# A two-layer decoder on one core: the routings' position matrices in another layout, the first norms' roots on Pool, and fewer waits at the last stop

## The reference

```
x += attention with mixed key halves (16 heads)        # layer 0
x += cross attention over 64 context rows (16 heads)
x += experts: 8 experts of 1024, top 2 of each token, at most 320 tokens an expert
x += retention (xpos turned queries and keys, decay, group norm)   # layer 1
x += cross attention
x += experts: 8 experts, top 2, relu, no limit
```

## Time and profile before

| | us |
|---|---|
| three runs: lowest, median, highest | 1706.25, 1707.44, 1709.11 |
| the profiled execution | 1711.54 |
| its span | 1709.7 |
| PE, DVE, ACT, POOL busy | 1563.4, 977.8, 583.6, 405.6 |

### The profile page before, as it was taken

How to read it: one execution, slowest core, us unless ns; L and a number is a source line. 1 busy time by engine, 2 the same in 40 slices (tenths; PEclk the granted TensorE clock), 3 DMA queues, 4 the chain that set the end, 5 groups by cost and what they waited for, 6 DMA issues and landing times. The chain is left out here.

```text
span 1709.7 us, 31257 instructions
## 1 busy us (share of the span) xinstructions
PE 1563.4 (91%) x10625; PEld 1105.4 (65%) x10626; DVE 977.8 (57%) x1754; ACT 583.6 (34%) x1161; POOL 405.6 (24%) x544
## 2 busy tenths in 40 slices
PE   6999999999989816999999999999989949999996
PEld 5734343343467615777777777865657649999995
DVE  6678888888679775122111221378879863444443
ACT  3277777777645400111111111033446500000000
POOL 1000000000122103142322211156652103333331
PEclk9999999999999957999999999999999969999998
DMA  2112221111411111133431331200024126666674
GB/s 75 38 44 68 57 57 47 42 47 42 158 32 38 50 44 41 16 96 105 105 87 28 96 87 16 65 1 2 1 79 157 50 91 180 176 176 180 181 183 118
DMA packets 89077, 134.90 MB, mean 79 GB/s; under 512 B 17568, under 2 KB 66080, under 8 KB 88832
## 3 DMA queue, kind: packets, MB, share of 16 engines
q1 hardware_dynamic: 73824, 113.05, 21.0%
q0 software_dynamic: 15168, 20.72, 7.6%
HBM read 98.00 MB, written 20.84 MB: 70 GB/s over the span
## 5 line engine op out<-in xcount | busy, mean ns | idle before, releaser
L2163 DVE TENSOR_REDUCE mx<-ps 128x1 f32<-128x1024 f32 x256 | 300.3, 1215 | 59.1 <-PE ps L2260 59.1
L1331 PE MATMUL ps<-xTe,wide 128*128 128x320 f32 x1024 | 277.6, 433 | 1.5 <-DVE hTe L1400 0.9
L1331 PEld LDWEIGHTS ps<-xTe,wide 128*128 128x128 f32 x1024 | 194.2, 190 | 82.3 <-DVE hTe L1400 1.4
L1400 DVE TENSOR_TENSOR hTe<-prT,ps 128x320 f32<-128x320 f32 x128 | 62.4, 488 | 213.5 <-ACT prT L1372 208.3
L2062 ACT ACTIVATE wide<-ps 128x512 f32<-128x512 f32 x256 | 139.3, 599 | 64.7 <-PE ps L2269 64.7
L2062 ACT ACTIVATE turns_of_use<-ps 128x512 f32<-128x512 f32 x256 | 139.6, 601 | 59.0 <-PE ps L2269 58.9
L2269 PE MATMUL ps<-QS,KS 99*128 99x512 bf16 x512 | 153.8, 381 | 0.7 <-ACT turns_of_use L2062 0.3
L1490 PEld LDWEIGHTS ps<-xw_all,w1t 128*128 128x128 f32 x1248 | 145.3, 192 | 3.6 <-issue 1.0
L1490 PE MATMUL ps<-xw_all,w1t 128*128 128x128 f32 x1248 | 145.8, 275 | 1.2 <-issue 0.7
L1372 ACT ACTIVATE prT<-ps 128x320 f32<-128x320 f32 x128 | 56.1, 438 | 261.7 <-PE ps L1331 260.0
L1507 PE MATMUL ps<-wide,hTm 128*128 x624 | 141.0, 379 | 0.0
(11 more groups left out here) (310 smaller groups left out, 2331.1 us busy)
## 6 DMA issues: line engine op xcount, KB each, us to landing
w1t<-in_L_ffn_w SPq DMA_DIRECT2D x39, 1024.0 KB
wide<-in_L_ffn_gate_weight SPq DMA_DIRECT2D x8, 1024.0 KB
wide<-_L_ffn_ff_pre_act_weight SPq DMA_DIRECT2D x8, 1024.0 KB
wide<-L_ffn_ff_post_act_weight SPq DMA_DIRECT2D x8, 1024.0 KB
wide<-in_L_ffn_w SPq DMA_DIRECT2D x1, 8192.0 KB, 27.3
QS<-wide SPq DMA_DIRECT2D x192, 32.0 KB, 2.0
KS<-wide SPq DMA_DIRECT2D x192, 32.0 KB, 2.0
VS<-V_all SPq DMA_DIRECT2D x32, 128.0 KB, 2.1
```

The costliest lines, as they stand in the source:

```text
L1331: ins = pe.matmul(ps[:, 3 + 2 * (q % 2) + n, 0:HC], wt[:, k, f * P:f * P + P], xTe[:, k, hf * HC:hf * HC + HC], start=(k == 0), stop=(k == ...
L1400: v.tensor_tensor(hTe[:, f, hf * HC:hf * HC + HC], sgt[:, q % 2, :], ps[:, 4 + 2 * (q % 2), 0:HC], ALU.mult).then_inc(f_m.sem, 1)
L2163: v.tensor_reduce(mx[:, s, t:t + 1], ps[:, 2 * (t % 2):2 * (t % 2) + 2, :], AX.XY, ALU.max).then_inc(h_rm.sem, 1)
```

## The change

Four things change. First, `one_hot`, `id_marks`, `gate_marks` and `hi_hot` get the tile (chunk) index innermost. What the comparison reads as a repeated single element before (step 0 in the innermost dimension) is now read along 16 or 32 neighbouring elements, and the numbers that it is compared with are laid out in full by Pool, once in each layer (`pool_numbers`, into `prT`, behind the last `x_av`). PE's operands become slices with a step: 16 elements for the stationary one, 32 for the moving one. Second, at the start Pool finishes the first norms' factors, in four parts of 2, 2, 4 and 8 tiles, the counters are raised in three portions around it, the memsets beside the values come behind `a_w`, ACT issues three of the loads and writes pair 1's rows, and DVE takes the last eight tiles' statistics one pair earlier. Third, the factors of the first two tiles of the retention are finished by Pool. Fourth, at stop 4 PE, ACT and DVE raise the counter without waiting for it.

```diff
@@ buffers @@
-            .rearrange("p (k t q) -> p k t q", k=2, t=NT)
+            .rearrange("p (k q t) -> p k q t", k=2, t=NT)
-        id_marks = marks[:, 0:2 * NT * 2 * NY].rearrange("p (c n h) -> p c n h", n=2, h=NY)
-        gate_marks = marks.rearrange("p (c n h) -> p c n h", n=3, h=NY)
-        hi_hot = ....rearrange("p (c h) -> p c h", h=NY)
+        id_marks = marks[:, 0:2 * NT * 2 * NY].rearrange("p (n h c) -> p n h c", n=2, h=NY)
+        gate_marks = marks.rearrange("p (n h c) -> p n h c", n=3, h=NY)
+        hi_hot = ....rearrange("p (h c) -> p h c", h=NY)
+        numbers = prT[:].rearrange("p h q -> p (h q)").bitcast(BF16)
+        q_numbers = numbers[:, 0:P * NT].rearrange("p (q t) -> p q t", t=NT)
+        h_numbers = numbers[:, P * NT:P * NT + NY * 2 * NT].rearrange("p (h c) -> p h c", h=NY)
@@ stops @@
+        def leave(eng):
+            eng.drain().then_inc(barrier, 1)
@@ pool_cross, one turn of its loop @@
+                if i == NP:
+                    pool.wait_ge(r_iota, 1)
+                    pool_numbers(pool, c, of(layer, NP - 1))
                 if here(i - 1):
                     end_factors(pool, c, i - 1, x_fid, x_fd, of(layer, i - 1))
@@ routing @@
-        chunks = lambda m: m.rearrange("p k t -> p (k t)").unsqueeze(2).to_broadcast([P, 2 * NT, NY])
+        chunks = lambda m: m.rearrange("p k t -> p (k t)").unsqueeze(1).to_broadcast([P, NY, 2 * NT])
+        def pool_numbers(pool, c, U):
+            pool.wait_ge(x_av.sem, x_av.upto(U))
+            c(pool.tensor_copy(q_numbers, iota_b[:].unsqueeze(2).to_broadcast([P, P, NT])))
+            pool.tensor_copy(h_numbers, tiles_b[:].unsqueeze(2).to_broadcast([P, NY, 2 * NT])).then_inc(r_numbers, 1)
         def dve_ids(v, c, layer, meanwhile):
-            v.wait_ge(r_iota, 1)
-            c(v.tensor_tensor(hi_hot, tiles_b[:].unsqueeze(1).to_broadcast([P, 2 * NT, NY]), chunks(hi_b[:]),
-                              ALU.is_equal))
-            v.tensor_scalar(id_marks[:, :, 0, :], hi_hot, row_no[:, 0:1], None, ALU.mult)
-            for k in range(2):
-                v.tensor_tensor(id_marks[:, k * NT:k * NT + NT, 1, :], hi_hot[:, k * NT:k * NT + NT, :],
-                                tiles_b[:, 0:NT].unsqueeze(2).to_broadcast([P, NT, NY]), ALU.mult)
+            v.wait_ge(r_numbers, layer + 1)
+            c(v.tensor_tensor(hi_hot, h_numbers, chunks(hi_b[:]), ALU.is_equal))
+            v.tensor_scalar(id_marks[:, 0, :, :], hi_hot, row_no[:, 0:1], None, ALU.mult)
+            v.tensor_tensor(id_marks[:, 1, :, :], hi_hot, chunks(tile_of[:]), ALU.mult)
             for k, made in ((0, r_rhs), (1, r_hot)):
-                v.tensor_tensor(one_hot[:, k, :, :], iota_b[:].unsqueeze(1).to_broadcast([P, NT, P]),
-                                lo_b[:, k, :].unsqueeze(2).to_broadcast([P, NT, P]), ALU.is_equal).then_inc(made, 1)
+                v.tensor_tensor(one_hot[:, k, :, :], q_numbers, lo_b[:, k, :].unsqueeze(1).to_broadcast([P, P, NT]),
+                                ALU.is_equal).then_inc(made, 1)
@@ pe_ids (pe_gates likewise) @@
-                ins = pe.matmul(ps[:, 0, 0:2 * NY], one_hot[:, i // NT, i % NT, :],
-                                id_marks[:, i, :, :].rearrange("p n h -> p (n h)"), ...
+                ins = pe.matmul(ps[:, 0, 0:2 * NY], one_hot[:, i // NT, :, i % NT],
+                                id_marks[:, :, :, i].rearrange("p n h -> p (n h)"), ...
@@ retention, DVE and then Pool @@
-            factors(*BACK[0])
+            begin_factors(v, *BACK[0], x_fia)
+            pool.wait_ge(x_fia.sem, x_fia.upto(NP))
+            finish_factors(pool, c, *BACK[0], e_fa)
@@ start, SP and then ACT @@
-            for dst, src in ((ident[:], ...), (qwB[:], ...), (wkA, ...), (wqA, ...), (wvA, ...)):
+            for dst, src in ((ident[:], w["c_ident"]), (wkA, chunked(w["L0_attn_Wk"]))):
+            for dst, src in ((qwB[:], ...), (wqA, ...), (wvA, ...)):
+                act.dma_start(dst, src).then_inc(w_part, 16)
...
+            act.wait_ge(a_fa.sem, a_fa.upto(1))
+            act.wait_ge(a_xn.sem, a_xn.upto(0))
+            act_rows(act, 1, xn[:, 1, :, :], a_xn)
@@ start, Pool @@
-            for s in sigs:
+            for s in sigs[0:12]:
                 pool.sem_inc(s.sem, LAG * s.per)
+            def factors_of(n):
+                pool.wait_ge(a_fi.sem, a_fi.upto(n))
+                finish_factors(pool, c, (0, 2, 4, 8)[n], (2, 4, 8, 16)[n], a_fa)
+            factors_of(0)
+            factors_of(1)
+            for s in sigs[12:50]:
+                pool.sem_inc(s.sem, LAG * s.per)
+            factors_of(2)
+            pool.wait_ge(a_w, 1)
             (the memsets beside the values, as before, with v_set)
+            for s in sigs[50:]:
+                pool.sem_inc(s.sem, LAG * s.per)
+            factors_of(3)
@@ start, DVE @@
-            factors_of(0, 1)
-            ln_rows(v, 0, 0, a_xn, a_tr)
+            stats_of(0, 2)
+            stats_of(2, 4)
             v.wait_ge(w_part, W_LOADS)
             (maximum and difference of the softmax weights, as before)
+            v.wait_ge(a_fa.sem, a_fa.upto(0))
+            ln_rows(v, 0, 0, a_xn, a_tr)
...
-            ln_rows(v, 1, 1, a_xn, a_tr)
             c(v.tensor_copy(identb[:], ident[:]))
-            factors_of(1, 2)
+            stats_of(4, 8)
+            v.wait_ge(a_xn.sem, a_xn.upto(1))
             for u in range(2, NP):
-                if u == 4:
-                    factors_of(2, 4)
+                if u == 3:
+                    stats_of(8, 16)
+                v.wait_ge(a_fa.sem, a_fa.upto(2 if u < 4 else 3))
                 ln_rows(v, u, u % 2, a_xn, a_tr)
@@ stop 4, on ACT, DVE and PE @@
-            meet(..., 4)
+            leave(...)
```

More of the change, by code:

```diff
@@ L471, in row_stats @@
             return ins
-        def norm_factors(v, c, t0=0, t1=NT):
-            for t in range(t0, t1):
-                ins = v.bn_aggr(mv[:, t, :], stats[:, t, :])
-            c(ins)
-            rsqrt(v, c, nv[:, :, t0:t1], mv[:, t0:t1, 1], LN_EPS)
         def norm_rows(v, out_, t):
@@ L1186, in pe_ids @@
                     pe.wait_ge(r_hot, layer + 1)
-                ins = pe.matmul(ps[:, 0, 0:2 * NY], one_hot[:, i // NT, i % NT, :],
-                                id_marks[:, i, :, :].rearrange("p n h -> p (n h)"), start=(i == 0), stop=(i == 2 * NT - 1))
+                ins = pe.matmul(ps[:, 0, 0:2 * NY], one_hot[:, i // NT, :, i % NT],
+                                id_marks[:, :, :, i].rearrange("p n h -> p (n h)"), start=(i == 0), stop=(i == 2 * NT - 1))
             ins.then_inc(r_sum, 1)
@@ L1193, in pe_gates @@
             for i in range(2 * NT):
-                ins = pe.matmul(ps[:, 7, 0:3 * NY], one_hot[:, i // NT, i % NT, :],
-                                gate_marks[:, i, :, :].rearrange("p n h -> p (n h)"), start=(i == 0),
+                ins = pe.matmul(ps[:, 7, 0:3 * NY], one_hot[:, i // NT, :, i % NT],
+                                gate_marks[:, :, :, i].rearrange("p n h -> p (n h)"), start=(i == 0),
                                 stop=(i == 2 * NT - 1))
@@ L1730, in rows_back @@
                 c(row_stats(v, BACK[n][0], BACK[n][1] - BACK[n][0]))
-            def factors(t0, t1):
-                norm_factors(v, c, t0, t1)
-                v.scalar_tensor_tensor(out=nmr[:, t0:t1], in0=mv[:, t0:t1, 0], scalar=-1.0, in1=nv[:, 0, t0:t1],
-                                       op0=ALU.mult, op1=ALU.mult).then_inc(e_fa.sem, 1)
             def masked(t, m):
@@ L2091, in _ @@
             act_cross(act, c, 1)
-            meet(act, 4)
+            leave(act)
             act.wait_ge(r_sub, 2)
@@ L2099, in _, with stats_of @@
             c = Chain(v, chain_dve)
-            def factors_of(q0, q1):
-                for q in range(q0, q1):
+            def stats_of(t0, t1):
+                for q in range(t0 // 4, (t1 + 3) // 4):
                     v.wait_ge(x_part[q], 16)
-                    for t in range(4 * q, 4 * q + 4):
-                        ins = v.bn_stats(stats[:, t, :], xr[:, t, :])
-                c(ins)
-                norm_factors(v, c, 4 * q0, 4 * q1)
-            factors_of(0, 1)
-            ln_rows(v, 0, 0, a_xn, a_tr)
+                c(row_stats(v, t0, t1 - t0))
+                begin_factors(v, t0, t1, a_fi)
+            stats_of(0, 2)
+            stats_of(2, 4)
             v.wait_ge(w_part, W_LOADS)
@@ L2215, in _ @@
             dve_cross(v, c, 1, scale_last, add_last)
-            meet(v, 4)
+            leave(v)
             dve_route1(v, c)
@@ L2374, in _ @@
             pe_cross(pe, 1, pe_retention(pe))
-            meet(pe, 4)
+            leave(pe)
             pe_count(pe, STEPS + 6)
```

32 lines of the change are left out of this document (14 added, 18 removed).

## The result

| | before | after |
|---|---|---|
| first comparison: median of 8 and 8 runs | 1707.81 | 1713.24, ratio 1.0028 [1.0015, 1.0041] |
| second comparison: 17 and 12 runs | 1710.71 | 1712.13, ratio 1.0011 [1.0001, 1.0020] |
| profiled execution, its span | 1711.54, 1709.7 | 1712.74, 1710.9 |
| PE, DVE, ACT, POOL busy | 1563.4, 977.8, 583.6, 405.6 | 1578.0, 958.0, 583.4, 419.8 |

The change made the kernel slower, by 0.1 to 0.3% (the second interval only just leaves 1 out). The forecast was 1694.5. DVE does 20 us less, and PE is busy for 15 us more.

The account below looks back on a forecast made before the run. PE, busy 1563.4 of 1709.7 us, was taken as the bound, with gains only in its waits. 3.0 + 1.4 + 3.4 + 2.5 + 3.4 + 0.2 - 1.0 = 12.9 gave 1698.6, at the median's level 1694.5 us; range 1689.5 to 1702.0.

Parts of the forecast that it names:

- PE's reads with a step: Ids' and gates' products in both routings: stepped operands cost 1.0 us, between nothing and 8.4 us.
- rival A: PE's gates' products at half speed: 1696.7 us, or 1700.5 if the ids also ran so; chance 0.22.
- The range: Whole kernel: 1689.5 to 1702.0 us, holding all but Rival D and the tails.
- The ids' gain: Both routings: packed comparisons on DVE make the ids ready 3.4 us earlier in each.
- Rival D: Ids and gates: PE's stepped reads cost three times or more, 1708.7 us, at four times 1714; chance 0.05.
- DVE's comparisons: Routings: two-input 16-bit instructions at 0.5 ns an element, 0.82 us for 1280 elements and 1.22 for 2048.
- Rival B: Routings: DVE gains nothing from the packing, both routings stay, 1700.3 us; chance 0.07.
- The start: First norms: PE's second turn at 11.1 instead of 14.14, 3.0 us, plus 1.4 us for the wait ahead of pair 4.
- Stop 4: Stop ahead of the second routing: DVE's 2.75 us wait goes, a 0.2 drain stays, 2.5 us gained.
- Pool's copies: Number tiles laid out by Pool once a layer: 3.3 us within 6.36 us of cover, nothing on the path.
- Retention: Retention's first two tiles: ACT has its first rows 0.9 us earlier, 0.2 us gained.
- The level: Whole kernel: the runs' median, 1707.44 us, lies 4.1 below the profiled 1711.54, taken off at the end.

Follow-up runs that it names:

- after_again: The changed kernel, unchanged, profiled a second time and timed again beside the kernel before: ratio 1.0011 [1.0001, 1.0020].
- before_again: The kernel before, unchanged, profiled a second time: 1707.92 us where the first profile took 1711.54.
- loads_on_sp: Changed kernel with only PE's loaded matrix stepped, streamed columns contiguous, and all five start loads issued by SP again: 1696.82 us, ratio 0.9920.
- experiment 4: ids_stepped: the changed kernel with gate_marks alone back to contiguous columns, the ids' marks still stepped: 1725.03 us, ratio 1.0082.
- step_probe: Changed kernel with the routings' old layout, plus 192 extra products at steps of 2 to 64 bytes: 16 products took 1.00 us at 2 bytes of column step, 3.42 at 64.
- gates_thrice: Changed kernel with only the loaded matrix stepped, streamed columns contiguous, and the gates' 32 products run three times: 1708.32 us, ratio 0.9974.
- pairs: Changed kernel with matrices laid out in pairs of tiles, so PE reads at 4-byte steps, and no Pool copies later: 1697.58 us, ratio 0.9907.

## Why the prediction was wrong, step by step

- **PE's reads with a step** is the step that failed: "I take 1.0". Measured in the profiles: ids 2.3 and gates 5.0 in each routing, 14.6 us of products; behind the gates 1.9 us (seven products of 0.53 us each, twice the usual) and 1.6 us (5.26 less 3.84, 0.60 less 0.39) for the clock, 0.5 and 2.2 in after_again's profile. In the second routing some of this replaced what stood there before: PE's wait of 0.51 us ahead of the gates is gone, and its fillers took 5.29 us instead of 6.15. I had set the upper bound at a third of the speed, "by these rows", but no row bore on it. The gates ran at 0.27 of theirs. The value was chosen near the lower bound because a product that "leaves no spare" looked like rival A at worst. The probe would have been needed; without it the two ends deserved the same weight.
- **The range** left this bound out. I wrote that the low values of every term give about 1700. With 8.4 for the reads in place of 1.0 and all else as in the sum it is 1701.9, with the low values of start and stop too 1704.8, and with DVE gaining nothing 1711.6.
- **What the profiles add up to**: a shift of -12.9 us was forecast, +1.2 measured, 14.1 apart. The ids' gain fell short by 4.6, the start by 1.0, the stop by 0.7; between the ids and the first blocks 12.1 went (7.0 with the stall at 678 taken out, and 5.1), where 1.0 stood in the sum. Against that stand about 3.5 us in which the first profile of the kernel before was late by chance (1.0 near 475, 1.0 near 1270, 1.5 at 678).
- **Rival D**, given 0.05, is what happened: it decides from 2.7 times, and at four times it gave 1714. That 1713.2 was measured is luck as a number. The ids' price was under its three times (1.9), the gates' above (3.7), it left out the clock, which was in none of my cases, and its sum at three times has 3.2 us for a half of the ids where three times 1.25 are 3.75; with that it is 1710.9 instead of 1708.7.
- **The Trainium skill's line rule**, from which I had worked out half speed and rival A, pointed the right way. It names no price, and my half was too mild: with one element in each line PE streams at 0.27 of its rate.
- **DVE's comparisons**: forecast 0.82 and 1.22, measured 0.83 and 1.2; 0.5 ns an element was a choice between two bounds, and it came out. Rival B is out. The 3.4 us a routing became 1.1, since DVE now waits for PE.
- **The start**: 4.4 forecast, 3.4 measured, 2.5 against before_again. The 1.51 us ahead of pair 4 went as forecast. The rows of pair 0 began at 9.13, past the 8.6 that I had named as a sign of being wrong, and the second turn came at 12.42, not 11.1: x landed 1.5 late instead of 0.4, and the last weights (SP's Wk) at 8.8, where I had taken at most 7.9. loads_on_sp gives half of the miss back. The slow step of the weights is gone (0.35 and 0.35), but the memsets that moved now stand beside pair 2's rows:

```profile
16.09 4.63 DVE L486 TENSOR_SCALAR xn<-xr,mv,nv 128x256 f32<-128x256 f32 x2 [2.02 <-issue]
16.31 3.94 POOL L2006 MEMSET V_all<- 128x240 f32 x16
20.78 0.66 PE L503 MATMUL ps<-ident,xn 128*128 128x128 f32 x4 [0.20 <-DVE xn L486]
```

Two row instructions take 4.63 us instead of 0.73, until Pool is done. PE was busy meanwhile and lost 0.20. I had said the memsets come "long before they are needed", and hadn't asked what runs beside them.

- **Stop 4**: 2.5 forecast; DVE's wait went as forecast, the lead grew by 1.8. The last router products ran at half clock this time, 1.88 us instead of 1.06, and took 0.8 of it:

```profile
1375.87 1.88 PE L918 MATMUL ps<-rw,xT 128*128 128x8 f32 x8 [0.67 <-ACT xT L584]
1378.10 0.29 DVE L1001 TENSOR_REDUCE tk<-lg 128x16 f32<-128x128 f32 x1
```

- **Pool's copies**: 3.3 forecast and hidden; 1.89 and 1.25 us, done 3.0 us ahead of the next factors. Right:

```profile
1365.66 1.89 POOL L1117 COPY prT<-iota_b 128x2048 bf16<-128x2048 bf16 x1 [4.99 <-PE ps L946]
1367.61 1.25 POOL L1118 COPY prT<-tiles_b 128x1280 bf16<-128x1280 bf16 x1
1371.83 0.20 POOL L752 TENSOR_TENSOR nv<-mv,eps 128x2 f32<-128x2 f32 x1 [2.96 <-DVE mv L670]
```

- **Retention**: 0.2 forecast, 0.2 measured (1109.40 to 1109.20, of a shift that was 0.0 ahead of it). ACT's first rows came 1.0 earlier (1107.76), 0.9 forecast.
- **The level**: I took 4.1 us off, since three runs had their median at 1707.44. The medians of 10 to 17 runs of the same kernel later were 1710.7 to 1713.0, so 1711.54 was no high time, and about 3 us of the distance between 1694.5 and 1713.2 are this step. Comparing two single profiles showed a change of 1.2 us (4.8 with before_again) where the medians showed 5.4 and then 1.4.

What stays open: how the changed kernel's loss splits between ids and gates in timed runs (experiment 4 missed it), and what in the second routing is the clock's share, which differs between executions. What held DVE, ACT and Pool until 678 in the first profile of the kernel before, and why Pool's gathers slow beside DVE's stepped write, no run here shows.

## What to carry to other kernels

When a layout is turned round for one engine, count the bytes between neighbours for every engine that reads it. Here two neighbours side by side gave DVE its packed rate and left PE's streamed columns at a step of 4 bytes, which is free (1.02 us for 1.00); more was loss only. Set each timed kernel against the runs of the kernel before that were taken beside it: bare times from different comparisons misled here by 2 to 3 us. And profile the kernel before twice before reading a shift of 1 us off it. An access that no row shows is better measured in idle time of the engine, as in step_probe, than placed between two bounds; and behind whatever gets slower on PE, look at the granted clock of the work that follows.

## What the runs showed of the hardware

- Streamed columns in bf16, 120 of them, 16 products: 1.00 us at a step of 2 bytes, 1.02 at 4, 1.90 at 8, 3.57 at 16, 3.64 at 32, 3.42 at 64. The loaded matrix: 1.00 at 2 bytes, 1.14 at 64. The slow products cost about 1.8 ns a column (150 ns for 80, 215 for 120) at either clock.
- The clock fell to 0.50 behind groups at 16 bytes and more with PE busy throughout, and stood at 1.00 behind those at 4 and 8; it stood at 1.00 through and behind 7.2 us of gates streamed at full rate (gates_thrice, first routing).
- DVE, two inputs of 16 bit: 0.65 ns an element or less (0.83 us for 1280, 1.2 for 2048) with neighbours side by side in all operands, also when only two are (pairs); 1.49 and 2.25 with a repeated innermost input. The Trainium skill ("VectorE: DVE Perf Modes", The perf-mode tier table) gives 1224 ns for 2048; measured 1219 (mean of the four in the changed kernel).
- DVE writing bf16 with 240 bytes between neighbours: 5.5 us for 1280 elements. Beside it Pool's indirect gathers took 4.9 to 5.2 us each instead of 1.0 (ids_stepped).
- Two one-input f32 instructions of DVE on 256 columns stood until Pool's 16 memsets were over, 4.63 us instead of 0.73. The Trainium skill ("SBUF — State Buffer", Terms) tells of a port pair that DVE and GpSimd lock against each other for a whole instruction; these rows agree in kind, and no run here separates it from other causes.
